# A gated delta-rule attention block and a top-1 column network on one core: the small matmuls in whole batches, gates and betas by Tanh, q and k scaled in place, a new order on all five engines

## The chip, the cores and the metric

One core of one Trainium2 chip. The metric is the device time of the kernel in microseconds. Engines are named as in the profile: PE is TensorE's matmuls, PEld its weight loads, DVE VectorE, ACT ScalarE, POOL GpSimd and SP SyncE, which issues nearly all transfers.

## The reference

Two residual layers over x of shape (4, 2048, 512), all in float32. The first is a recurrent attention with 16 heads of 32 channels, the second a network of 16 columns of which each token uses one.

```python
q, k, v, gate = ((x @ W.T).reshape(b, l, 16, 32) for W in (Wq, Wk, Wv, Wg))
beta = sigmoid(x @ Wb.T).reshape(b, l, 16, 32)
alpha = exp(-exp(A_log) * softplus(x @ Wa.T + dt_bias))          # one per head
q = q / norm(q) / sqrt(32);  k = k / norm(k)
def step(S, (k_t, q_t, v_t, beta_t, a_t)):                        # over time, S is 32x32 per head
    S = S * a_t
    S = S + k_t[:, None] * ((v_t - k_t @ S) * beta_t)[None, :]
    return S, q_t @ S
ctx = rmsnorm(ys) * norm_w * silu(gate);  attn = ctx @ Wo.T + bo
x = x + layernorm(attn(layernorm(x)))
logits = cosine(x, col_emb) + sigmoid(gelu(x @ gate_w1 + gate_b1) @ gate_w2 + gate_b2)
y = softmax weight of the best column * gelu(x @ W_cols[best] + b) @ proj_w[best] + proj_b + x
x = x + layernorm(layernorm(y) * ln_g + ln_b)                     # ffn of layernorm(x)
```

## The kernel before

**Stages.** A main stage goes through the sequence in 32 blocks of 64 time steps for all four batch rows, so 256 tokens a block. A second stage, after it, takes the tokens sorted by their column in 80 groups of 128 rows. The change is in the main stage.

**The main stage.** Each engine runs its own `step(...)` 35 times. A step holds work of four blocks at once: `chain` is the recurrence of block b, `ahead` the projections and decays of the next block, `after` the outputs of the one before, `late` the column choice of the one before that. 31 of the steps have both `chain` and `ahead`. The order of work in a step is written out by hand on each engine; semaphores join them.

**The recurrence** runs in two chunks of 32 time steps, with a state S of 32x32 for each of 16 groups (`G`) on each of four partition quarters, so 64 small products make one batch. There are six kinds: `key_products` (L469), `state_to_u` (L477), `first_half_to_u` (L485), `state_to_outputs` (L492), `chunk_to_outputs` (L497), `change_state` (L504). Each batch is issued in two halves of 32 products (`on_tiles(half, ...)`), and other PE work stands between most halves. Each product is a float32 matmul on a 32x32 part of the array and appears in the trace as two matmuls and two weight loads: a half is 64 matmuls, a batch is 128 matmuls and 128 weight loads. Between the products DVE solves a triangular system column by column (`solve_half`, L1145 to L1160), four times a step, and adds the state (`add_to_state`, L1165).

**Large matmuls.** `project` (L437) makes q, k, v, beta and gate from xT, with 256 columns each; `squares_sum` (L446), `decays` (L522), `log_alpha` (L511), `output_projection` (L535), `outputs_squares_sum` (L530), `turn` (L454, transposes), `gate_hidden` (L543), `gate_logits` (L553, L556) and `ranks` (L565 to L571) are the rest. They share three PSUM banks (`work`), given out in the order of the list `TURNS`: `into` makes PE wait until the bank's last use has been read (`READ_BY`).

**ACT** copies PSUM out: `copy_and_square` (L802, qraw and its square), `inverse_norm` (L809), `copy_decays` (L816), `copy_outputs` (L792, frees uq), `copy_turned` (L796), `copy_values` (L839). `sigmoid` (L835) makes beta and the gate's sigmoid `sg`, from another table than Ln and Exp; the statistics (`token_norm`, `length_of_normed`) and Gelu (L910) change tables again, each change an ACT_TABLE_LOAD. DVE multiplies `sg` by the gate in PSUM (L1281, L1290) and q and k by their inverse norms (`scale`, L1171).

**POOL** multiplies pairs of rows by beta (`pairs_times_beta`, L992), decays state, k and q (L976, L981, L1003), adds the residual (L1039) and scatters rows to DRAM (L1019). **SP** writes `Ak` to DRAM and fetches it back broadcast over partitions (`fetch_pairs`), loads tokens and stores outputs. Its queue order is `fetch_pairs(0,1)`, residual, `write_rows(1)`, `fetch_pairs(1,0)`, `fetch_pairs(1,1)`, `load_tokens`, `write_rows(0)`, `store`, `fetch_pairs(0,0)`.

## Time and profile before

| what | value |
| --- | --- |
| time, median of 3 runs | 3433.52 us (3429.26 to 3442.22) |
| the profiled execution's own time | 3454.87 us |
| its span in the profile | 3453.1 us |
| PE busy | 3006.9 us, 87% |
| PEld busy | 2295.4 us, 66% |
| DVE busy | 2357.6 us, 68% |
| ACT busy | 1824.4 us, 53% |
| POOL busy | 1913.1 us, 55% |
| mean granted clock of PE | 0.912 |

The span runs from the first to the last instruction. Busy times of engines overlap each other. PE and PEld are two sides of one engine: a weight load can run while a matmul does. In the profile, an idle time is followed by an arrow and what ended it; "issue" stands where the engine waited for nothing that the profile shows. The main stage fills the span from its first microseconds to about 3050 us.

### The profile page before, as it was taken

The page shows a single profiled execution, that of the slowest core. Times are in us where ns is not written, and L with a number is a line of the kernel's source. Part 1 is how long each engine was busy: PE and PEld are TensorE (multiplying, and loading weights), DVE is VectorE, ACT ScalarE, POOL GpSimd, SP SyncE. Part 2 cuts the span into 40 slices and gives each one's busy share as a digit, 9 for nine tenths or more (in the row PEclk, how much of TensorE's full clock was granted, in tenths as well). Part 3 has the DMA queues.
Part 4 walks back from the last instruction along what each step waited for, and adds up shares of the span by engine and source line. Part 5 has one row for each costly group of instructions (what it writes and reads, how often), then busy time and mean ns, then how long its engine had stood idle before and what let it go on. Part 6 is the DMA issues. An engine that isn't in the chain of part 4 may idle for free.

```text
span 3453.1 us, 141658 instructions
## 1 busy us (share of the span) xinstructions
PE 3006.9 (87%) x59368; PEld 2295.4 (66%) x59368; DVE 2357.6 (68%) x10708; ACT 1824.4 (53%) x4154; POOL 1913.1 (55%) x2903
## 2 busy tenths in 40 slices
PE   4899999999999999999999999999999999637774
PEld 4667777777777777777777777777777777414443
DVE  1667666666666766777666666666666677657896
ACT  2355555555555555555555555555555555326664
POOL 1555565455555555555565555555556555416887
PEclk9899999999999999999999999999999999759997
DMA  3544444544444445444444454444445444545773
GB/s 112 132 119 115 113 117 112 124 117 108 118 115 114 117 121 124 112 113 117 115 117 112 124 124 110 114 115 115 116 116 124 124 111 118 142 141 105 132 126 65
DMA packets 350030, 404.87 MB, mean 117 GB/s; under 512 B 31169, under 2 KB 293953, under 8 KB 348881
## 3 DMA queue, kind: packets, MB, share of 16 engines
q1 hardware_dynamic: 332752, 362.10, 42.1%
q0 software_dynamic: 16640, 33.71, 5.4%
q8 instruction: 468, 7.67, 1.0%
q14 instruction: 170, 1.38, 0.1%
HBM read 323.97 MB, written 75.93 MB: 116 GB/s over the span
## 4 chain that ended last, share of the span: by engine, by line
PE 62%; ACT 20%; DVE 11%; issue 4%; POOL 1%; ACTq 1%; DMA 1%; POOLq 0%; SPq 0%; DVEq 0%
PE work L437 25%; PE work L535 7%; PE work L543 3%; PE work L446 3%; DVE uk L1158 3%; DVE Ut L1155 3%; PE su L504 3%; PE work L454 2%; PE uq L497 2%; PE uk L477 2%; PE kkq L469 2%; PE uq L492 2%; PE work L530 2%; PE work L522 2%; PE work L511 2%
## 5 line engine op out<-in xcount | busy, mean ns | idle before, releaser
L437 PE MATMUL work<-xT,w_sb 128*128 128x256 f32 x5120 | 1314.1, 407 | 6.5 <-ACT beta L835 5.1
L992 POOL TENSOR_TENSOR pairs<-pairs,beta 128x240 f32<-128x240 f32 (+14 forms) x1920 | 862.4, 488 | 667.0 <-ACT beta L835 380.9
L437 PEld LDWEIGHTS work<-xT,w_sb 128*128 128x128 f32 x5120 | 996.3, 202 | 183.8 <-issue 31.1
L1158 DVE TENSOR_TENSOR uk<-uk,Ut 128x120 f32<-128x120 f32 (+14 forms) x3840 | 708.6, 226 | 1.1
L1155 DVE TENSOR_TENSOR Ut<-pairs,uk 128x120 f32<-128x120 f32 (+14 forms) x3840 | 688.2, 215 | 5.5 <-POOL pairs L992 5.0
L802 ACT ACTIVATE qraw<-work 128x512 f32<-128x512 f32 x128 | 75.9, 593 | 432.2 <-DVE kq L1171 305.5
L1165 DVE TENSOR_TENSOR S<-Sd,su 128x512 f32<-128x512 f32 x64 | 44.0, 687 | 359.1 <-PE su L504 359.1
L535 PE MATMUL work<-wo_sb,ctxT 128*128 128x512 f32 x512 | 240.6, 613 | 6.3 <-POOL ctxT L1011 6.3
L1003 POOL TENSOR_TENSOR kd<-kd,dec 128x512 f32<-128x512 f32 x64 | 68.0, 1084 | 258.8 <-DVE kd L1237 258.8
L492 PEld LDWEIGHTS uq<-kqd,S 32*32 32x32 f32 x8192 | 90.7, 114 | 156.8 <-ACT oT L792 105.8
L1145 DVE TENSOR_TENSOR uk<-vT,uk 128x128 f32<-128x128 f32 x256 | 62.9, 291 | 187.7 <-PE uk L485 115.8
L492 PE MATMUL uq<-kqd,S 32*32 32x32 f32 x8192 | 105.6, 203 | 95.7 <-ACT oT L792 93.4
L809 ACT ACTIVATE qr<-work 128x512 f32<-128x512 f32 x128 | 75.9, 593 | 193.9 <-PE work L446 191.5
L1017 POOL TENSOR_TENSOR xfw<-xfw,pb_sb 128x1024 f32<-128x1024 f32 x32 | 75.5, 2359 | 175.7 <-DVE slot L1224 175.7
L535 PEld LDWEIGHTS work<-wo_sb,ctxT 128*128 128x128 f32 x512 | 93.7, 193 | 105.4 <-issue 94.8
L1171 DVE TENSOR_TENSOR kq<-qraw,qr 128x512 f32<-128x512 f32 x128 | 136.1, 1082 | 35.0 <-ACT qr L810 35.0
L839 ACT ACTIVATE vT<-work 128x512 f32<-128x512 f32 x64 | 38.2, 597 | 224.5 <-PE work L437 224.5
L981 POOL TENSOR_TENSOR kqd<-kq,eg 128x1024 f32<-128x1024 f32 x64 | 150.3, 2349 | 3.8 <-DVE kq L1171 3.8
L976 POOL TENSOR_TENSOR Sd<-S,eg_end 128x512 f32<-128x512 f32 x64 | 67.9, 1061 | 148.6 <-DVE S L1165 148.6
L446 PE MATMUL work<-qsq,squares 128*128 128x512 f32 x256 | 147.0, 658 | 0.0
L469 PEld LDWEIGHTS kkq<-kq 32*32 32x32 f32 x8192 | 119.1, 105 | 34.1 <-issue 29.8
L1194 DVE TENSOR_TENSOR lt<-work,gb_sb 128x32 f32<-128x32 f32 x32 | 6.1, 191 | 195.7 <-PE work L556 195.7
(249 smaller groups left out, 5970.8 us busy)
## 6 DMA issues: line engine op xcount, KB each, us to landing
pairs<-pair_rows SPq DMA_DIRECT2D x512, 256.0 KB, 3.5
pairs<-pair_rows SPq DMA_DIRECT2D x512, 224.0 KB, 3.7
xt<-in_x SPq DMA_DIRECT2D x66, 256.0 KB, 5.4
pair_rows<-Ak SPq DMA_DIRECT2D x64, 256.0 KB, 2.3
x<-in_x SPq DMA_DIRECT2D x64, 256.0 KB, 4.8
out<-x SPq DMA_DIRECT2D x64, 256.0 KB, 3.7
wo_sb<-xs_rows SPq DMA_DIRECT2D x30, 258.0 KB, 2.9
w_sb<-in_w_in SPq DMA_DIRECT2D x1, 5120.0 KB, 14.9
```

The lines of the kernel that those rows point to most:

```text
L437: mm = pe.matmul(w[:, half * BT:(half + 1) * BT], w_sb[:, f, j * D + hg * P:j * D + (hg + 1) * P], xT[:, f, :], start=(f == 0), stop=(f == ...
L446: pe.matmul(w, blk1, qsq[n % 2][:], start=True, stop=True).then_inc(s["ss_full"], 1)
L469: on_tiles(half, "kkq_full", lambda g, q, q_half: pe.matmul(kkq[q, g], kq[q, g, c, 0, :], kq[q, g, c].rearrange("p a t -> p (a t)"), start ...
L492: on_tiles(half, None, lambda g, q, q_half: pe.matmul(uq[q, g], S[q, g, :], kqd[c][q, g, 1, :], start=(g == 0), stop=True, skip_group_chec ...
L504: on_tiles(half, "su_full", lambda g, q, q_half: pe.matmul(su[q, g, :], kd[c][q, g, :], delT[c][q, g, :], start=True, stop=True))
L535: mm = pe.matmul(w, flat(ctxT[:, hg * B + tb * BL:hg * B + (tb + 1) * BL, :]), wo_sb[:, hg, :], start=(hg == 0), stop=(hg == KD - 1))
L543: mm = pe.matmul(w[:, n * BT:(n + 1) * BT], gw1_sb[:, f, n * P:(n + 1) * P], xfT[:, f, :], start=(f == 0), stop=(f == KD - 1))
L981: link(nc.gpsimd.tensor_tensor(kqd[c][:], kq[:, :, c], eg[:, :, c * C:(c + 1) * C].unsqueeze(2).to_broadcast([P, G, 2, C]), ALU.mult), "kq ...
L992: ins = nc.gpsimd.tensor_tensor(a, a, beta[:, :, t:t + WID[t0]], ALU.mult)
L1155: link(v.tensor_tensor(Ut[:, g, 0:n], pr[:, g], uk[:, g, at:at + 1].to_broadcast([P, G // 2, n]), ALU.mult), "vb_free" if i and (c, j, t0) ...
L1158: link(v.tensor_tensor(uk[:, g, at + 1:at + 1 + n], uk[:, g, at + 1:at + 1 + n], Ut[:, g, 0:n], ALU.subtract), f"pairs_free{j}" if i and t ...
L1171: link(v.tensor_tensor(unit(kq, hp)[:, :, :, 1 - j, :], per_chunk(qraw[n % 2][:]), per_chunk(qr[n % 2][:]), ALU.mult), "kq_ready", hold=(n ...
```

## The change

- **PE.** `on_tiles` loses its halves: each kind is one batch of 64 products. In a step the batches stand in four runs: `change_state(1)`, `chunk_to_outputs(1)` at the end of a step and `state_to_u(0)`, `key_products(1)`, `state_to_outputs(0)` at the start of the next, five in a row; `first_half_to_u(0)` alone; `change_state(0)`, `chunk_to_outputs(0)`, `state_to_u(1)`, `state_to_outputs(1)`, four in a row; `first_half_to_u(1)`, `key_products(0)`, two in a row. The number of products stays. `chunk_to_outputs(1)` moves to its own step. `TURNS` is reordered, and alpha lies in the bank of the logits.
- **ACT.** One change to the table with Tanh and Gelu and one back in each step. Sigmoid becomes 0.5 * tanh(x/2) + 0.5 for beta (two instructions for each half); the gate is copied to `silu`, its tanh goes to `xn`, and DVE makes (tanh + 1) * gate, with the missing half put into `nw`. q and k go from PSUM straight into `kq`; new waits guard `kq`, `dec`, `xn` and `beta` (for beta, all of POOL's pair products of the block).
- **DVE.** `scale` works in place in `kq`; the decays are turned from `dec`, which takes the place of `gsb`; `decay_products(0)` stands inside `solve_half(1, 1)`; other parts are reordered.
- **POOL.** The decay differences go ahead of the scatter, and half of the last pair products ahead of the residual.
- **SP.** `load_tokens` goes ahead of `fetch_pairs(1,1)`, `store` ahead of `write_rows(0)`.

```diff
-    ("logits",), ("xT", 0), ("xT", 1), ("qk", 0), ("rms", 0), ("rms", 1), ("alpha",), ("qk", 1), ("ss", 0),
-    ("qk", 2), ("wo", 0), ("wo", 1), ("rank",), ("ss", 1), ("G", 0), ("G", 1), ("qk", 3), ("ss", 2),
-    ("gate", 0), ("ss", 3), ("gate", 1), ("beta", 0), ("beta", 1), ("xfT", 0), ("xfT", 1), ("v", 0), ("v", 1),
-    ("hid",),
+    ("xT", 0), ("xT", 1), ("rms", 0), ("rms", 1), ("qk", 0), ("logits",), ("qk", 1), ("ss", 0), ("qk", 2), ("ss", 1),
+    ("G", 0), ("G", 1), ("wo", 0), ("wo", 1), ("rank",), ("ss", 2), ("qk", 3), ("gate", 0), ("ss", 3), ("gate", 1),
+    ("beta", 0), ("beta", 1), ("xfT", 0), ("xfT", 1), ("v", 0), ("v", 1), ("hid",),
 ]
 BANK = {use: n % NW for n, use in enumerate(TURNS)}
+BANK["alpha",] = BANK["logits",]
...
+   rank="rank_read", gate="gate_read", beta="beta_read", v="v_read", xfT="xfT_ready", hid="h_ready",
...
-        qraw = [sb(f"qraw{n}", [P, GU * T]) for n in range(2)]
         qsq = [sb(f"qsq{n}", [P, GU * T]) for n in range(2)]
-        qr = [sb(f"qr{n}", [P, GU * T]) for n in range(2)]
-        sg = sb("sg", [P, GU * T])
+        qr = [sb(f"qr{n}", [P, GU * T]) for n in range(4)]
...
-        gsb = qsq[1][:], ctx_flat[:, 0:GU * T]
-        gT = qraw[1][:], ctx_flat[:, GU * T:2 * GU * T]
+        gT = gate_t = [xn[:, hp, :] for hp in range(2)]
...
+    if ahead:
+        load_tokens(following)
+    if chain:
         fetch_pairs(1, 1)
-    if ahead:
-        load_tokens(following)
...
-def on_tiles(half, full, product):
-    for g in range(half * GU, (half + 1) * GU):
+def on_tiles(product):
+    for g in range(G):
         for h in range(HP):
             mm = product(g, slice(DH * h, DH * h + DH), slice(DH * h, DH * h + CS))
-    if half and full:
-        mm.then_inc(s[full], 1)
...
-def state_to_u(c, half):
-    if not half:
-        take(pe, "kqd_ready")
-        take(pe, "S_ready")
-    on_tiles(half, "uk_full", lambda g, q, q_half: pe.matmul(
-        uk[q, g], S[q, g, :], kqd[c][q, g, 0, :], start=(g == 0), stop=True, skip_group_check=True))
...
+    take(pe, "kqd_ready")
+    take(pe, "S_ready")
+    on_tiles(lambda g, q, q_half: pe.matmul(
+        uk[q, g], S[q, g, :], kqd[c][q, g, 0, :], start=(g == 0), stop=True, skip_group_check=True))\
+        .then_inc(s["uk_full"], 1)
...
 def step(p, chain, after, ahead, late):
     if chain:
-        state_to_u(0, 0)
-    if late:
-        gate_logits(0)
-    if chain:
-        state_to_u(0, 1)
-    if late:
-        gate_logits(1)
+        state_to_u(0)
+        key_products(1)
+        state_to_outputs(0)
     if ahead:
         take(pe, "xn_ready", TB)
         turn("xT", xn, 0)
         turn("xT", xn, 1)
     if after:
-        chunk_to_outputs(NC - 1, 0)
-        chunk_to_outputs(NC - 1, 1)
+        outputs_squares_sum(0)
+        outputs_squares_sum(1)
     if ahead:
         take(pe, "xT_ready", 2)
         project("qk", 0, 0, 0)
+    if late:
+        gate_logits(0)
+    if ahead:
         project("qk", 0, 0, 1)
-    if chain:
-        key_products(1, 0)
-        key_products(1, 1)
-    if after:
-        outputs_squares_sum(0)
-        outputs_squares_sum(1)
-    if ahead:
-        log_alpha(0)
-    if chain:
-        first_half_to_u(0, 0)
-    if ahead:
-        log_alpha(1)
+    if late:
+        gate_logits(1)
+    if ahead:
+        log_alpha(0, late)
+        log_alpha(1, late)
         project("qk", 0, 1, 0)
+        project("qk", 0, 1, 1)
+    if chain:
+        first_half_to_u(0)
+    if ahead:
...
-    if chain:
-        first_half_to_u(0, 1)
-    if ahead:
-        project("qk", 0, 1, 1)
         project("qk", 1, 0, 0)
-    if chain:
-        state_to_outputs(0, 0)
-    if after:
-        take(pe, "ctx_ready", 2)
-        output_projection(0)
-    if chain:
-        state_to_outputs(0, 1)
-    if ahead:
         project("qk", 1, 0, 1)
-    if chain:
-        change_state(0, 0)
-    if after:
-        output_projection(1)
-    if chain:
...
         squares_sum(1)
         take(pe, "lax_ready")
         decays(0)
         decays(1)
-    if chain:
-        state_to_u(1, 0)
-    if ahead:
+    if after:
+        take(pe, "ctx_ready", 2)
+        output_projection(0)
+        output_projection(1)
+    if chain:
+        change_state(0)
+        chunk_to_outputs(0)
+        state_to_u(1)
+        state_to_outputs(1)
+    if late:
+        ranks()
+    if ahead:
+        squares_sum(2)
         project("qk", 1, 1, 0)
-    if chain:
-        state_to_u(1, 1)
-    if ahead:
         project("qk", 1, 1, 1)
-        squares_sum(2)
...
         project("gate", 4, 0, 0)
-    if chain:
-        chunk_to_outputs(0, 0)
-    if ahead:
+        project("gate", 4, 0, 1)
         squares_sum(3)
-        project("gate", 4, 0, 1)
-    if chain:
-        chunk_to_outputs(0, 1)
-    if ahead:
         project("gate", 4, 1, 0)
         project("gate", 4, 1, 1)
+    if chain:
+        first_half_to_u(1)
+    if ahead:
         take(pe, "kq_ready", 4)
-        key_products(0, 0)
+        key_products(0)
         project("beta", 3, 0, 0)
-        key_products(0, 1)
         project("beta", 3, 0, 1)
-    if chain:
-        first_half_to_u(1, 0)
-    if ahead:
         project("beta", 3, 1, 0)
-    if chain:
-        first_half_to_u(1, 1)
+        project("beta", 3, 1, 1)
...
-    if ahead:
-        project("beta", 3, 1, 1)
-    if chain:
-        state_to_outputs(1, 0)
-    if after:
         turn("xfT", xfw, 1)
     if ahead:
         project("v", 2, 0, 0)
-    if chain:
-        state_to_outputs(1, 1)
-    if ahead:
         project("v", 2, 0, 1)
+    if ahead:
         project("v", 2, 1, 0)
-    if chain:
-        change_state(1, 0)
+        project("v", 2, 1, 1)
     if after:
         take(pe, "xfT_ready", 2)
         gate_hidden()
     if chain:
-        change_state(1, 1)
-    if ahead:
-        project("v", 2, 1, 1)
+        change_state(1)
+        chunk_to_outputs(1)
...
+def load_tanh_gelu():
+    nc.scalar.preload_act_table_set("gelu_and_others")
...
-    take(act, "kq_ready", free=2)
+    j, hp = divmod(n, 2)
     take(act, "qk_full")
-    nc.scalar.activation(qraw[n % 2][:], bank("qk", n), ACT.Copy)
+    nc.scalar.activation(unit(kq, hp)[:, :, :, 1 - j, :], per_chunk(bank("qk", n)), ACT.Copy)
     link(nc.scalar.activation(qsq[n % 2][:], bank("qk", n), ACT.Square), "q_sq_ready")
...
-    link(nc.scalar.activation(gsb[hp], w, ACT.Copy), "g_copied")
+    link(nc.scalar.activation(flat(unit(dec, hp)), w, ACT.Copy), "g_copied")
...
-def sigmoid(name, hp, dst):
-    take(act, name + "_full")
-    return nc.scalar.activation(dst, bank(name, hp), ACT.Sigmoid)
+def copy_gate(p, hp):
+    take(act, "gate_full")
+    link(nc.scalar.activation(flat(unit(silu[1 - p], hp)), bank("gate", hp), ACT.Copy), "gate_read", hold=True)
+def gate_tanh(p, hp):
+    nc.scalar.activation(gate_t[hp], flat(unit(silu[1 - p], hp)), ACT.Tanh, scale=0.5).then_inc(s["gate_ready"], 1)
+def beta_sigmoid(hp):
+    b = flat(unit(beta, hp))
+    take(act, "beta_full")
+    link(nc.scalar.activation(b, bank("beta", hp), ACT.Tanh, scale=0.5), "beta_read", hold=True)
+    link(nc.scalar.activation(b, b, ACT.Identity, scale=0.5, bias=half[:]), "beta_ready")
...
     if ahead:
+        take(act, "gate_used", 2, free=2)
         norm_tokens(xn, xt, x_rn, "xn_ready")
+    if after:
+        square_outputs(0)
+        square_outputs(1)
+    if ahead:
         copy_turned("xT", xT, 0)
         copy_turned("xT", xT, 1)
-    if late:
-        take(act, "lg_ready")
-        nc.scalar.activation(lt[:, 1], lt[:, 1], ACT.Exp, scale=-1.0).then_inc(s["sig_ready"], 1)
-    if after:
-        copy_outputs(NC - 1)
-        square_outputs(0)
-        square_outputs(1)
-    if ahead:
-        copy_and_square(0)
     if after:
         inverse_rms(0)
         inverse_rms(1)
...
-    if after:
-        take(act, "ctx_raw", 2)
-    if ahead:
+        take(act, "kt_ready", 2, free=2)
+        take(act, "kqd_ready", 2, free=2)
+        copy_and_square(0)
+    if late:
+        take(act, "lg_ready")
+        nc.scalar.activation(lt[:, 1], lt[:, 1], ACT.Exp, scale=-1.0).then_inc(s["sig_ready"], 1)
+    if ahead:
+        copy_and_square(1)
         inverse_norm(0)
-        copy_and_square(1)
         copy_and_square(2)
+        inverse_norm(1)
+        take(act, "kd_ready", 2, free=2)
+        copy_decays(0, 1 - p)
+        copy_decays(1, 1 - p)
...
+    if after:
+        take(act, "ctx_raw", 2)
+    if chain:
+        copy_outputs(0)
+    if ahead:
+        inverse_norm(2)
+        copy_and_square(3)
     if after:
         take(act, "y_mv_ready")
         token_norm(y_rn, y_mv)
...
         pair_decays(1)
-        inverse_norm(2)
+        copy_gate(p, 0)
         inverse_norm(3)
-        take(act, "gate_used", free=1)
-        link(sigmoid("gate", 0, sg[:]), "gate_ready")
-        take(act, "gate_used", free=1)
-        link(sigmoid("gate", 1, sg[:]), "gate_ready")
+        copy_gate(p, 1)
...
     if after:
         take(act, "x1_mv_ready")
         token_norm(x1_rn, x1_mv)
         norm_tokens(xfw, x1, x1_rn, "xf_ready")
-        length_of_normed(x1_mv, x1_rn)
-    if chain:
-        copy_outputs(0)
-    if after:
-        copy_turned("xfT", xfT, 0)
+    if ahead:
+        take(act, "x_mv_ready")
+        token_norm(x_rn, x_mv)
+    load_tanh_gelu()
     if ahead:
         if chain:
             take(act, "vb_free")
-        link(sigmoid("beta", 0, flat(unit(beta, 0))), "beta_ready")
-        link(sigmoid("beta", 1, flat(unit(beta, 1))), "beta_ready")
+            take(act, "pr_ready", 8)
+        beta_sigmoid(0)
+        beta_sigmoid(1)
...
+        gate_tanh(p, 0)
+        gate_tanh(p, 1)
+    if after:
+        copy_turned("xfT", xfT, 0)
+        copy_turned("xfT", xfT, 1)
+    if ahead:
         copy_values(0)
-    if after:
...
             link(nc.scalar.activation(hT[n], bank("hid")[:, n * BT:(n + 1) * BT], ACT.Gelu, bias=gb1_sb[:, n:n + 1]), "h_ready")
+    if chain:
+        copy_outputs(1)
     load_ln_exp()
-    if ahead:
-        copy_values(1)
-        take(act, "x_mv_ready")
...
+def pairs_times_beta(c, j, parts=(0, 1)):
+    for n in parts:
...
+    if chain:
+        decay_state(p, 1)
+        pairs_times_beta(1, 1, (0,))
...
-        decay_state(p, 1)
-        pairs_times_beta(1, 1)
+        pairs_times_beta(1, 1, (1,))
...
-        link(v.tensor_tensor(uk[:, g, h], uk[:, g, h], beta[:, g, th], ALU.mult), behind=1)
+    for i, g in enumerate(turns):
+        link(v.tensor_tensor(uk[:, g, h], uk[:, g, h], beta[:, g, th], ALU.mult),
+             "vb_free" if i and (c, j) == (NC - 1, 1) else None, behind=1, hold=True)
...
-    link(v.tensor_tensor(unit(kq, hp)[:, :, :, 1 - j, :], per_chunk(qraw[n % 2][:]), per_chunk(qr[n % 2][:]), ALU.mult), "kq_ready", hold=(n == 1))
+    link(v.tensor_tensor(unit(kq, hp)[:, :, :, 1 - j, :], unit(kq, hp)[:, :, :, 1 - j, :], per_chunk(qr[n][:]), ALU.mult), "kq_ready")
...
+def gate_values(p, hp):
+    half_silu = flat(unit(silu[1 - p], hp))
+    take(dve, "gate_ready")
+    link(v.scalar_tensor_tensor(half_silu, gate_t[hp], 1.0, half_silu, ALU.add, ALU.mult), "gate_used")
...
+        normed_outputs(1)
     if ahead:
...
-    if ahead:
-        take(dve, "kqd_ready", 2, free=2)
...
+    if ahead:
+        for hp in range(2):
+            take(dve, "g_copied")
+            link(v.transpose(gT[hp], flat(unit(dec, hp))), "gT_ready")
...
+    if after:
+        for tb in range(TB):
+            token_stats(y, y_mv, tb, "y_mv_ready")
     if ahead:
         scale(1)
-        take(dve, "g_copied")
-        link(v.transpose(gT[0], gsb[0]), "gT_ready")
-        take(dve, "g_copied")
...
-        take(dve, "gate_ready")
-        link(v.tensor_tensor(flat(unit(silu[1 - p], 0)), bank("gate", 0), sg[:], ALU.mult), "gate_used")
...
     if ahead:
+        next_tokens_stats()
+    if ahead:
         take(dve, "dec_ready", 2)
+    if chain:
+        take(dve, "corr_full")
+        solve_half(1, 1, {2: lambda: decay_products(0)} if ahead else {})
+    elif ahead:
         decay_products(0)
-        take(dve, "gate_ready")
-        link(v.tensor_tensor(flat(unit(silu[1 - p], 1)), bank("gate", 1), sg[:], ALU.mult), "gate_used")
-        next_tokens_stats()
-    if chain:
-        take(dve, "corr_full")
-        solve_half(1, 1)
+    if ahead:
+        gate_values(p, 0)
+        gate_values(p, 1)
+    if chain:
         add_to_state()
...
```

## Rows read from the trace of the kernel before

**Rows 1.** The page, busy time of each engine over the span

```profile
PE 3006.9 (87%) x59368; PEld 2295.4 (66%) x59368; DVE 2357.6 (68%) x10708; ACT 1824.4 (53%) x4154; POOL 1913.1 (55%) x2903
```

**Rows 2.** Windows: one step; us, busy of each engine, PEclk, DMA share, GB/s

```profile
1506.24:1598.30 92.06, 84.71 (x1829) 65.92 (x1821) 63.87 (x316) 50.50 (x112) 51.51 (x78) 0.94 0.47 116
```

**Rows 3.** Waits over the whole span: us in total, times, longest us

```profile
DVE S L1165 <- PE su L504: 359.1, 33, 12.2
...
PE uq L492 <- ACT oT L792: 93.4, 31, 3.4
...
PE work L454 <- ACT beta L835: 46.6, 30, 1.8
...
PE uk L477 <- issue: 26.0, 52, 1.7
```

**Rows 4.** Timeline of PE: start us, us, instruction, idle before

```profile
1517.26 1.89 PE L437 MATMUL work<-xT,w_sb 128*128 128x256 f32 x8
1519.08 0.75 PE L497 MATMUL uq<-Aq,delT 32*32 32x32 f32 x64
1519.76 1.12 PE L446 MATMUL work<-qsq,squares 128*128 128x512 f32 x2
...
1529.82 1.10 PE L469 MATMUL kkq<-kq 32*32 32x64 f32 x64
1530.85 1.99 PE L437 MATMUL work<-xT,w_sb 128*128 128x256 f32 x8
1532.77 0.73 PE L485 MATMUL uk<-Ak,delT 16*32 16x16 f32 x64
...
1573.06 1.99 PE L469 MATMUL kkq<-kq 32*32 32x64 f32 x128
1574.97 1.99 PE L530 MATMUL work<-y,squares 128*128 128x512 f32 x4
```

**Rows 5.** Timeline of PEld in a middle step

```profile
1563.06 0.97 PEld L553 LDWEIGHTS work<-ceT,xfT 128*128 128x128 f32 x8 [1.07 <-issue]
1563.95 0.53 PEld L556 LDWEIGHTS work<-gw_sb,pairs 128*128 128x128 f32 x4
1564.31 1.55 PEld L454 LDWEIGHTS work<-squares,xn 128*128 128x128 f32 x8
1566.19 1.57 PEld L497 LDWEIGHTS uq<-Aq,delT 32*32 32x32 f32 x108 [0.33 <-issue]
1569.10 0.27 PEld L497 LDWEIGHTS uq<-Aq,delT 32*32 32x32 f32 x20 [1.33 <-issue]
```

**Rows 6.** Timeline of PEld in the last `chain` step

```profile
2946.04 0.73 PEld L497 LDWEIGHTS uq<-Aq,delT 32*32 32x32 f32 x76 [0.21 <-issue]
2946.67 0.10 PEld L469 LDWEIGHTS kkq<-kq 32*32 32x32 f32 x1
2946.68 0.10 PEld L497 LDWEIGHTS uq<-Aq,delT 32*32 32x32 f32 x1
2946.68 0.79 PEld L469 LDWEIGHTS kkq<-kq 32*32 32x32 f32 x50
2950.06 1.04 PEld L469 LDWEIGHTS kkq<-kq 32*32 32x32 f32 x48 [2.59 <-issue]
```

**Rows 7.** DMA queues in that middle step: packets, MB, share of 16 engines

```profile
q8 instruction: 14, 0.23, 1.1%
```

**Rows 8.** Windows beside a clock change, columns as in rows 2

```profile
1561.10:1564.55 3.45, 2.49 (x80) 2.35 (x80) 0.00 (x0) 2.90 (x8) 3.45 (x7) 1.00 0.86 192
1564.55:1567.97 3.42, 3.35 (x116) 2.89 (x115) 3.25 (x19) 1.31 (x3) 3.42 (x10) 0.50 0.55 118
...
2980.00:3000.00 20.00, 5.08 (x241) 4.33 (x241) 16.08 (x95) 8.54 (x29) 13.95 (x21) 0.53 0.72 191
```

**Rows 9.** Lines: table loads of ACT; busy us, mean ns, idle before

```profile
L835 ACT ACT_TABLE_LOAD x62 | 79.5, 1283 | 16.4 <-PE work L437 15.8
```

**Rows 10.** Timeline of DVE: first and last instructions of one `solve_half`

```profile
1514.71 0.49 DVE L1145 TENSOR_TENSOR uk<-vT,uk 128x128 f32<-128x128 f32 x2 [1.86 <-PE uk L477]
...
1523.97 0.72 DVE L1160 STREAM_TRANSPOSE delT<-uk 128x512 f32<-128x512 f32 x1
```

153 lines of the change are left out of this document (70 added, 83 removed).

## The prediction

> **What bounds the kernel now.** I read the busy shares first [rows 1]: PE leads with 87%, DVE has 68%, ACT and POOL under 56%. The windows view of one middle step (from one `ranks` to the next) gives 92.06 us with 84.71 busy on PE [rows 2]; DVE works 63.87 of it, ACT 50.50, POOL 51.51. So a step costs PE's work plus 7.35 us in which PE stands still. The waits show where other engines have room: DVE stood 359.1 us before the state add, waiting for PE, while PE's own large waits are 93.4 us before `state_to_outputs` (uq not yet copied by ACT) and 46.6 us before the transposes of xfw (a bank not yet read by ACT's sigmoid) [rows 3]. What sets the end of each step is PE, in program order.
>
> The next question is what small batches cost. In PE's timeline a half batch takes 0.68 us from its first matmul to the next work (1519.08 to 1519.76) and a `key_products` half 1.03 (1529.82 to 1530.85) [rows 4]. A whole batch is 1.36 and 1.91 us (1573.06 to 1574.97). That is 256 PE instructions in 1.4 to 1.9 us, and they must be brought in. The queue that carries instructions moved 14 packets, 0.23 MB, in the step, 16 KB each [rows 7], for 1829 + 1821 = 3650 matmuls and weight loads [rows 2]: one packet for 3650 / 14 = 261, so 256 with the few other instructions that PE has. The stalls called "issue" lie at exactly this distance. After the stall that ends at 1563.06 there come 8 + 4 + 8 + 108 = 128 weight loads, so 256 instructions, and then PEld stands 1.33 us until 1569.10 in the middle of a batch [rows 5]. In the last `chain` step, where the large matmuls between are missing, the same is seen bare: from 2946.04 PEld does 76 + 1 + 1 + 50 = 128 loads and stands 2.59 us until 2950.06, a period of 4.02 us for 256 instructions, in the middle of `key_products` [rows 6]. I read this as follows: the packet after next is asked for only when PE enters the next one, and takes about 4 us to be usable. Small batches between large matmuls hide it; 14 packets in 92 us is one in 6.6 us on average. Small batches in a row would not.
>
> **The change, part by part, for one of the 31 full steps.**
>
> *Switches between small and large work, gained.* A `key_products` batch in one piece saves 2 x 1.03 - 1.91 = 0.15 us. Eight large matmuls behind a small batch take 1.92 us (1530.85 to 1532.77), behind a large one 1.82 (1517.26 to 1519.08) [rows 4], so 0.10 more. Each switch out and back costs 0.25. Before there are 22 stretches of small work in a step (ten batches in two pieces, two in one), after it 4, so 18 x 0.25 = 4.5 us. Bounds: 1.8 us with only the 0.10, 6 us if the smaller batches save more than the wide one.
>
> *PE's waits, gained.* 93.4 / 31 = 3.0 us for uq: `chunk_to_outputs` now has a whole batch or two behind it before `state_to_outputs`, which covers ACT's copy. 46.6 / 31 = 1.5 us for the bank, as its reader moves. 26.0 / 31 = 0.8 us of "issue" at `state_to_u` [rows 3], counted anew below. Together 5.3; bounds 0.8 and 7.35, all idle time [rows 2].
>
> *Instructions, lost.* A batch is exactly one packet. In a run of n batches n packet borders are crossed; the packet behind the first was fetched during slow work, the other n - 1 must wait. The runs are 5, 1, 4 and 2 batches: 4 + 0 + 3 + 1 = 8 waits. Each packet takes 4.02 us [rows 6] in place of the batch's own 1.36, or 1.91 for the two `key_products` among them: 6 x 2.66 + 2 x 2.11 = 20.2 us. Bounds for one wait: 1.33 us, the stall seen in a middle step [rows 5], so 10.6 a step; above, 6.04 - 1.36 = 4.7, if the 6.04 us between the two stalls of that step were all fetch, so 37. Nothing at all is a rival. I take the bare period since it has little slow work in it, as the new runs have.
>
> *Clock, lost.* The granted clock fell to 0.50, the 1.2 GHz level, in the stretch behind one that had small batches and a stall in it (PE busy 2.49 of 3.45), and stood at 0.53 over 20 us with PE busy 5.08 [rows 8]. Starved runs of 20, 16 and 8 us will be at the low level; small batches don't feel it, but the large matmuls just behind each run do, for one or two such stretches of 3.4 us, at half speed: 1.7 to 3.4 us, three times, 5 to 10. The step already loses some: a mean of 0.94 [rows 2] is (1 - 0.94) x 92 / 0.5 = 11 us at the low level, some 4 us of it lost in dense work. Net +3; bounds 0 and +7.
>
> *Dependences.* Inside a run the state add (0.7 us on DVE) and ACT's copy of uq are behind a 4 us packet, so they cost nothing; without the starvation the state add after `change_state` is still covered by the 1.36 us of `chunk_to_outputs`, nearly. A `solve_half` takes 1514.71 to 1524.69, 10.0 us [rows 10]. Between `state_to_u(0)` and `first_half_to_u(0)` PE now has two batches and some 15 us of large work; between `state_to_u(1)` and `first_half_to_u(1)` one batch and 14 us, where DVE also has `rows_of_tokens`, two token statistics and a scale ahead of the solve: about even. I book +1 for it. The beta wait on all eight pair products holds ACT, with xfT, v and the hidden layer queued behind; PE has 15 us of `first_half_to_u`, `key_products` and beta before the bank, so nothing, up to 3 us.
>
> *ACT.* Some 6 table loads fewer, 1.283 us each [rows 9], against two gate copies and two more passes for beta: it is not what ends a step, so nothing beyond the waits above. In-place scaling, the dec turn on DVE and the new SP order are likewise off PE's path: DVE has 28 us free a step [rows 2]. `load_tokens` now goes ahead of `fetch_pairs(1,1)` and waits for the decays, `write_rows(0)` waits behind the store; both stand ahead of pair products needed more than 10 us later. Zero, up to 2 us.
>
> Sum: -4.5 - 5.3 + 20.2 + 3 + 1 = +14.4 us a step, x 31 = +446. The second stage and the ends are untouched. The profiled execution took 3454.87 us, so 3901; the median of the runs is 0.994 of that execution (3433.52 / 3454.87), so about 3875.
>
> **The rivals.**
>
> *Instructions are not what binds (faster).* PE gets packets early enough in the new runs, either since it holds more than two or since they can overlap. Then a step is 92.06 - 4.5 - 5.3 + 1 = 83.3: 31 x -8.8 = -273, so 3182, 3162 as a median. For it: in most of the step's borders nothing is lost, and `issue` is only 26.0 us at `state_to_u` [rows 3]. Against it: two stalls 256 instructions apart [rows 5, 6], each in the middle of a batch where no semaphore is. The point from which it decides is a period of about 2.4 us for a packet: 8 waits of (2.4 - 1.5) would be all that the gains of 8.8 allow beside the clock. The Trainium skill states this rival as a rule (Runtime: NRT & Kernel Launch, Instruction fetch mechanics): PE's instruction memory holds 2048 instructions, refilled in blocks of 256, and the refill is mostly hidden. By that rule a run of 1280 instructions would be in store and the sum would be this rival's; the trace agrees with the block of 256 and not with the depth. 10%.
>
> *A smaller wait (slower by less).* The wait is 1.33 us as in the middle step [rows 5]: 10.6 in place of 20.2, a step of +4.8, +149 in all, 3582 as a median. 10%.
>
> *Gains and losses cancel.* Waits of 1.33 us, no clock loss and the upper bound of the switches give -6 - 5.3 + 10.6 + 1 = 0.3 a step. 5%.
>
> **How the numbers follow.** The forecast, waits near 2.5 us each, has 75%. The range takes in the smaller wait and reaches 3560 below; above, 5 us a step over the forecast for slower packets in a busy step and the clock's upper bound, so 4050. A measurement of this kernel can tell about 0.5% from no change. Slower 75 + 10, same 5, faster 10.
>
> **What would show it.** A step (one `ranks` to the next) near 106 us; weight loads of the runs in pieces of 128, each begun 4 us behind the last with an idle time of 2 to 2.7 us put down to "issue"; eight of them a step; uq's wait on ACT gone; granted clock below 0.9 in the middle; still 14 instruction packets a step; eight table loads down to two. I am wrong if whole batches follow each other at 1.4 us, or if a wait of PE on DVE or POOL over 3 us stands in every step.

## The result, and the profile after

The changed kernel takes 3838.53 us (median of 4 runs, 3828.82 to 3844.84) against 3435.88 us (3429.26 to 3442.22) for the kernel before: a ratio of 1.117 [1.1137, 1.1202]. It is slower by about 400 us, and the forecast was 3875. A step of the main stage, from one `ranks` to the next, takes 104.7 us in the mean of the middle ones, where it took 92.2: 12.5 us more, and 31 such steps are 388 us. So nearly all of it comes from the steps, and they are read below. The trace of the kernel before is of an execution of 3454.87 us, 19 us above this median (0.6 us a step), so the 12.5 us are low by about that much.

The page's busy times and granted clock, the kernel after:

```profile
PE 3059.7 (80%) x59368; PEld 2459.9 (64%) x59368; DVE 2357.2 (61%) x10710; ACT 1657.7 (43%) x4103; POOL 1903.2 (50%) x2903
PEclk9788888888888887788888888887888888767998
...
PE 69%; issue 15%; DVE 9%; ACT 4%; POOL 1%; ACTq 1%; DMA 0%; DVEq 0%; POOLq 0%
```

PE is the busiest still, and it is busy 53 us longer than in [rows 1], but its share fell from 87% to 80% because the span grew. The last line, the chain that ended last by engine, gives 15% to "issue", time in which an engine waits for nothing that the profile shows. No other engine became the bound: all shares fell.

PE's waits name what the idle time is. Engine, line and what it waited for: us in total, times, longest. First the main part of the main stage (548.6 to 3250 us, 25.8 steps):

```profile
PE uk L473 <- issue: 114.7, 51, 3.4
PE uq L493 <- issue: 114.1, 48, 4.5
PE uq L488 <- issue: 95.5, 50, 3.8
PE kkq L465 <- issue: 83.1, 48, 2.9
PE kkq L465 <- DVE kq L1158: 6.9, 6, 1.7
```

The first four rows are 407.4 us in 197 stalls: 7.6 stalls a step, 2.07 us each, 15.8 us a step; with two small rows more, at L528 and L481, "issue" is 16.0 us a step, where it was 1.1. All four stand at lines of small batches. What another engine causes is 0.6 us a step. The waits for ACT's copy of uq and for the bank, 4.5 us a step before [rows 3], have no row left that counts; with the wait for the next tokens' norm, what PE waited for ACT was 5.0 us a step before.

Where a stall stands is seen in the weight loads of the run of four batches (start, us, the group, idle time before):

```profile
1589.65 1.16 PEld L501 LDWEIGHTS su<-delT,kd 32*32 32x32 f32 x127 [0.76 <-issue]
...
1590.73 0.76 PEld L493 LDWEIGHTS uq<-Aq,delT 32*32 32x32 f32 x75
1593.66 0.73 PEld L493 LDWEIGHTS uq<-Aq,delT 32*32 32x32 f32 x50 [2.17 <-issue]
...
1594.30 1.11 PEld L473 LDWEIGHTS uk<-kqd,S 32*32 32x32 f32 x73
1597.84 0.78 PEld L473 LDWEIGHTS uk<-kqd,S 32*32 32x32 f32 x51 [2.42 <-issue]
...
1601.58 0.83 PEld L488 LDWEIGHTS uq<-kqd,S 32*32 32x32 f32 x53 [1.95 <-issue]
```

The three long idle times (2.17, 2.42, 1.95 us) are inside batches, where no semaphore is. Between the first and the second there are 50 + 2 + 2 + 73 = 127 weight loads, and a record can be missing: 256 instructions, as in [rows 5, 6]. The stretches begin 4.18 and 3.74 us apart. Over 24 middle steps there are 108 such distances inside runs, 3.36 to 5.95 us, 4.07 in the mean. The run of five, in PE's own timeline, has four:

```profile
1543.06 0.70 PE L493 MATMUL uq<-Aq,delT 32*32 32x32 f32 x36 [2.22 <-issue]
...
1547.91 0.70 PE L473 MATMUL uk<-kqd,S 32*32 32x32 f32 x36 [2.93 <-issue]
...
1553.58 1.18 PE L465 MATMUL kkq<-kq 32*32 32x64 f32 x36 [2.53 <-issue]
...
1557.05 0.76 PE L488 MATMUL uq<-kqd,S 32*32 32x32 f32 x39 [1.01 <-issue]
...
1559.50 3.62 PE L528 MATMUL work<-y,squares 128*128 128x512 f32 x4
```

The last row stands behind the run, with only eight transposes between: four matmuls of 512 columns in 3.62 us, where the same four took 1.99 us before [rows 4]. That is the clock. The windows view gives it by stretch: the whole step, the run of five, the stretch behind it, the work up to the run of four, that run, the stretch behind it. Columns: us; busy time of PE, PEld, DVE, ACT, POOL; granted clock; DMA share; GB/s.

```profile
1497.60:1602.47 104.87, 87.47 (x1812) 71.13 (x1810) 63.35 (x314) 44.84 (x110) 51.79 (x78) 0.81 0.42 102
1538.79:1557.73 18.94, 10.25 (x641) 9.58 (x640) 9.62 (x63) 5.28 (x8) 10.58 (x21) 0.60 0.48 111
1557.73:1563.04 5.31, 5.31 (x20) 3.24 (x14) 3.61 (x9) 2.51 (x4) 2.11 (x2) 0.50 0.24 57
1563.04:1589.65 26.61, 26.61 (x253) 20.00 (x251) 15.22 (x84) 13.15 (x36) 9.88 (x18) 1.00 0.44 106
1589.65:1602.47 12.82, 6.64 (x513) 6.21 (x512) 3.30 (x7) 0.60 (x1) 5.01 (x4) 0.66 0.54 131
1602.47:1607.41 4.94, 4.94 (x19) 3.63 (x15) 2.73 (x10) 1.02 (x2) 1.94 (x1) 0.50 0.03 6
```

The full 26.61 us without a gap, large work but for the one batch `first_half_to_u(0)`, run at 1.00. The two starved runs take 31.8 us of the step for 16.9 busy ones, and each is followed by some 5 us of dense work at 0.50, the 1.2 GHz level. The step's mean clock is 0.81, against 0.94 in [rows 2].

### The profile page after: what moved, and what is told of

Read it like the earlier page. It is cut to its first block, busy times and chain, and to the rows that moved or that the text cites. A ratio compares the mean times of both kernels' runs of the same rounds, so it can differ in the third digit from the quotient of the medians.

```text
span 3836.3 us, 141487 instructions
## 1 busy us (share of the span) xinstructions
PE 3059.7 (80%) x59368; PEld 2459.9 (64%) x59368; DVE 2357.2 (61%) x10710; ACT 1657.7 (43%) x4103; POOL 1903.2 (50%) x2903
## 4 chain that ended last, share of the span: by engine, by line
PE 69%; issue 15%; DVE 9%; ACT 4%; POOL 1%; ACTq 1%; DMA 0%; DVEq 0%; POOLq 0%
PE work L435 27%; PE work L533 6%; PE kkq L465 5%; PE uq L488 3%; PE work L541 3%; PE uk L473 3%; PE work L444 3%; PE uq L493 2%; PE work L452 2%; PE work L528 2%; PE su L501 2%; PE uk L481 2%; DVE uk L1145 2%; DVE Ut L1142 2%; PE work L509 1%
## 5 line engine op out<-in xcount | busy, mean ns | idle before, releaser
L435 PE MATMUL work<-xT,w_sb 128*128 128x256 f32 x5120 | 1250.4, 403 | 6.1 <-ACT beta L811 2.5
L435 PEld LDWEIGHTS work<-xT,w_sb 128*128 128x128 f32 x5120 | 1034.6, 204 | 243.7 <-issue 88.4
L977 POOL TENSOR_TENSOR pairs<-pairs,beta 128x240 f32<-128x240 f32 (+14 forms) x1920 | 861.8, 485 | 662.5 <-DMA pairs<-pair_rows 662.2
L465 PE MATMUL kkq<-kq 32*32 32x64 f32 x8192 | 221.1, 282 | 107.8 <-issue 99.7
L465 PEld LDWEIGHTS kkq<-kq 32*32 32x32 f32 x8192 | 197.2, 151 | 123.5 <-issue 112.1
L473 PE MATMUL uk<-kqd,S 32*32 32x32 f32 x8192 | 126.0, 223 | 146.4 <-issue 142.8
L1004 POOL TENSOR_TENSOR dec<-dec,xn 128x512 f32<-128x512 f32 x64 | 81.8, 1278 | 323.3 <-DVE xn L1259 323.3
L493 PE MATMUL uq<-Aq,delT 32*32 32x32 f32 x8192 | 106.5, 204 | 148.3 <-issue 148.3
L473 PEld LDWEIGHTS uk<-kqd,S 32*32 32x32 f32 x8192 | 112.3, 136 | 155.0 <-issue 151.3
L493 PEld LDWEIGHTS uq<-Aq,delT 32*32 32x32 f32 x8192 | 93.2, 114 | 152.1 <-issue 152.0
L767 ACT ACTIVATE kq<-work 128x512 f32<-128x512 f32 x128 | 75.8, 592 | 234.9 <-PE work L435 234.7
```

Of the source, the lines that this page charges most:

```text
L435: mm = pe.matmul(w[:, half * BT:(half + 1) * BT], w_sb[:, f, j * D + hg * P:j * D + (hg + 1) * P], xT[:, f, :], start=(f == 0), stop=(f == ...
L465: on_tiles(lambda g, q, q_half: pe.matmul(kkq[q, g], kq[q, g, c, 0, :], kq[q, g, c].rearrange("p a t -> p (a t)"), start=True, stop=True))\
L473: on_tiles(lambda g, q, q_half: pe.matmul(uk[q, g], S[q, g, :], kqd[c][q, g, 0, :], start=(g == 0), stop=True, skip_group_check=True))\
L493: on_tiles(lambda g, q, q_half: pe.matmul(uq[q, g], delT[c][q, g, :], Aq[c][q, g, :], start=False, stop=True, skip_group_check=True))\
L977: ins = nc.gpsimd.tensor_tensor(a, a, beta[:, :, t:t + WID[t0]], ALU.mult)
L1004: link(nc.gpsimd.tensor_tensor(d, d, gT[hp], ALU.subtract))
```

## The experiments

The theory: PE's instructions arrive in packets of 256, one ahead, and the next takes 3.5 to 4 us to be usable; batches in a row need one in every 1.4 us. The rivals: the new order on the other engines holds PE up, whole batches are slower in themselves, or the packets wait behind the data traffic. Every kernel was timed with the kernel before on the same chip, and only those ratios are compared. `spread` with `before_whole`, `supply` and `supply_traffic` ran on one chip (before: 3454.77 us), the rest on another (3433 us). One kernel's ratio still differed by 1.3% between the two (`before_whole`), so a difference of ratios below that isn't read across them.

**Spread: all of the change, but no two batches in a row.** The edit moves calls of PE's step, and three calls of ACT and DVE so that their waits stay covered. The four runs become twelve single batches with large work between.

```diff
     if chain:
         state_to_u(0)
-        key_products(1)
-        state_to_outputs(0)
...
+    if chain:
+        key_products(1)
...
+    if chain:
+        state_to_outputs(0)
...
     if chain:
         change_state(0)
-        chunk_to_outputs(0)
+    if after:
+        output_projection(1)
+    if chain:
         state_to_u(1)
-        state_to_outputs(1)
...
+    if chain:
+        change_state(1)
     if ahead:
         project("v", 2, 1, 0)
         project("v", 2, 1, 1)
+    if chain:
+        chunk_to_outputs(1)
...
-    if chain:
-        change_state(1)
-        chunk_to_outputs(1)
...
```

> The changed kernel with its whole batches kept, but no two of them in a row: 3 to 7 us of large matmuls stand between any two (ACT's two copies of uq and one DVE addition move along). Supply theory (PE gets 256 instructions, one batch, per 3.5 to 4 us, and stalls when it needs them sooner): the idle time put down to issue falls from 15.9 us a step to under 2, a step from 104.7 us to 84 to 90, the whole to 3200 to 3400 us. Rival (what costs is the new work on ACT and DVE and its waits, not the rows of batches): the step stays above 98 us, the whole above 3630.

Measured: 3375.31 us, 0.9775 [0.9748, 0.9802] of the kernel before, a step of 89.9 us. The loss of 11.7% became a gain of 2.2% with every operation kept. Its batches are whole and in one piece in the timeline, and its waits (500 to 2850 us, 26.1 steps) are of another kind:

```profile
1598.66 1.29 PE L473 MATMUL uk<-kqd,S 32*32 32x32 f32 x128
...
1606.99 1.99 PE L465 MATMUL kkq<-kq 32*32 32x64 f32 x128
```

```profile
PE work L452 <- ACT xn L726: 61.1, 26, 2.6
PE uk L481 <- DVE delT L1156: 43.0, 25, 2.6
PE work L452 <- ACT beta L820: 21.4, 17, 2.2
PE uk L473 <- issue: 17.3, 19, 2.2
```

"Issue" at small and large lines together is down to 1.7 us a step. In its place stand waits for the norm of the next tokens (2.3 us a step), for the solve (1.6 and more) and for the bank (0.8). Together the waits for other engines are 5.5 us a step, as much as in the kernel before (5.0) and far above the 0.6 of the change, where a late PE hides them.

**Before, whole batches in the old order.** This is the half that the change was to win from.

```diff
 def on_tiles(half, full, product):
-    for g in range(half * GU, (half + 1) * GU):
+    if not half:
+        return
+    for g in range(G):
```

> The kernel before, with nothing changed but that the first half of each small batch is issued with its second half: 12 stretches of small work a step in place of 22, each still between large matmuls. If a switch costs 0.25 us as the prediction worked out: 10 x 0.25 = 2.5 us a step, 78 in all, about 3358 us (ratio 0.977). If a switch costs nearly nothing, as the balance of the changed kernel's step suggests: 0 to -0.7 us a step, ratio 0.993 to 1.00. If whole batches already meet the supply limit here: slower.

> The kernel before with whole batches once more, for its trace, since its time was the same as before (1.0014). If a switch really costs 0.25 us, PE's small batches take 2.5 us a step less and another wait has grown by as much. If a switch costs nothing, batches and large matmuls take the same time as before, and no wait has changed.

> The kernel before with whole batches, timed again, as the first time (1.0014) and the look's step (90.2 us against 92.2) disagree. The look's trace: small batches 2.5 to 3.3 us a step less, the wait for uq gone (3.0), the wait for xfT's bank up from 1.5 to 5.9. If the look was right: ratio 0.975 to 0.985. If the gain is only moved: 0.995 to 1.003.

Measured: on the first chip 3462.98 us, 1.0014 [0.9996, 1.0031], just above the range that was given for a switch that costs nothing; on the second 3396.64 us in a single run (before 3433.08) and 3398.44 us in five rounds, 0.9888 [0.9868, 0.9909], between the two ranges expected. The two chips differ by 1.3%. On the second, the profile of the five-round kernel (500 to 2850 us) has

```profile
PE work L454 <- ACT beta L837: 150.3, 26, 6.2
PE uk L479 <- issue: 16.9, 17, 2.2
```

The uq wait of [rows 3] is gone (3.0 us a step) and the bank wait rose from 1.5 to 5.8 us, because PE arrives there earlier. All of PE's waits together are 8.0 us a step (6.1 before), and the step is 90.4 us, so PE's own work is 82.4 us in place of 86.0. Of these 3.6 us, 1.0 is clock (large matmuls spend 6.4 us a step at the low level, before 8.4). The other 2.6 us are put down to the ten switches that this kernel leaves out (12 stretches of small work for 22), 0.26 each. That is an upper estimate: the trace of the kernel before is of an execution of 3454.87 us, 21 us above the 3433.63 of this chip, 0.7 us a step; without it 0.19 is left for each. Why the first chip shows no gain stays open, since no comparable profile of this kernel is at hand from there.

**Supply: the same series of instructions alone.** This kernel computes something else: PE multiplies one loaded tile, eight batches of 64 small products with 0, 2, 4, 8 and 16 large products behind each, and no other engine works meanwhile. Its second form lets SP load 2 MB at a time without a pause.

```diff
+BIG = (0, 2, 4, 8, 16)
+ROUNDS = 8
...
+            for n in BIG:
+                large(40)
+                for _ in range(ROUNDS):
+                    batch()
+                    if n:
+                        large(n)
```

> Another computation: five series of 8 small batches (128 matmuls and 128 weight loads each, no semaphore inside), with 0, 2, 4, 8 and 16 large float32 products of 256 columns behind each batch, 40 of them ahead of each series, and no other transfer. Supply theory: at 0 a batch comes every 3.5 to 4.0 us, at 2 (about 0.9 us of large work) the same, at 4 still about 4, at 8 (3.6 us) it is the work itself, 5.1, and at 16 8.8; ahead of a series two packets are in store, so the first stall comes after one to two batches. Rival (PE or its memory is slow on small matmuls in a row, or more packets are held than two): at 0 a batch takes 1.4 us, or the first eight do.

Measured, from the end of one stall to the end of the next: 3.45 to 3.73 us at 0 large products (3.56 in the mean of five), 3.45 to 4.00 at 2 (3.77 of six), 3.45 to 3.73 at 4 (3.54 of six). At 8 large products a batch and what follows it take 4.87 us and at 16 they take 8.32, without a stall. The weight loads at 0, then at 8:

```profile
23.46 2.44 PEld L56 LDWEIGHTS small<-a 32*32 32x32 f32 x272 [0.33 <-issue]
28.18 1.18 PEld L56 LDWEIGHTS small<-a 32*32 32x32 f32 x128 [2.28 <-issue]
...
157.44 1.18 PEld L56 LDWEIGHTS small<-a 32*32 32x32 f32 x128 [0.33 <-issue]
158.66 3.32 PEld L60 LDWEIGHTS big<-a 128*128 128x128 f32 x16
```

After 40 large products the first 272 loads, 544 instructions, come freely: the rest of a packet and what was fetched. From there on every 128 loads, 256 instructions, cost 3.45 to 4.00 us, whatever fills them: at 2 and 4 large products the large work is nearly free. Counted through all 6080 weight loads of the run, each of its 15 stalls over 0.36 us after the start stands at 96 more than a multiple of 128. Nor does the period follow the clock: the 128 loads take 1.18 us at the high level and 1.80 at the low one (granted clock 0.50 from 31.6 to 35.0 us), and both periods are 3.45 us; the slower batch only leaves a shorter stall. No semaphore, no transfer of data and no other engine is in this, so the packet explains the stall by itself. At 8, 288 instructions take 4.87 us, 4.3 us for 256, and nothing is lost. The two readings bound the point on a quiet chip: under 3.45 us of work for 256 instructions PE stands, at 4.3 it does not.

**Supply under traffic.** The edit turns the loads on.

```diff
-TRAFFIC = False
+TRAFFIC = True
```

> The same with 2 MB loads issued one behind the other by SP all the time. If the time of a packet is mostly its own round trip: the period at 0 grows by under 15%. If it waits behind other transfers: over 4.5 us, which would make the 4.7 us periods of the changed kernel's steps a matter of its data traffic.

Measured, beside some 238 GB/s of loads: from stall to stall 4.96 us in the mean at 0 large products (single periods 3.73 to 6.75), and for 256 instructions 5.5 at 2 and 5.3 at 4. From one batch's start to the next it is 6.31 in the mean at 8 (4.87 without a stall, single ones 8.21 and 11.6), and 8.32 at 16, as without traffic.

```profile
37.47 1.80 PEld L56 LDWEIGHTS small<-a 32*32 32x32 f32 x128 [4.95 <-issue]
41.20 1.80 PEld L56 LDWEIGHTS small<-a 32*32 32x32 f32 x128 [1.93 <-issue]
47.39 1.79 PEld L56 LDWEIGHTS small<-a 32*32 32x32 f32 x128 [4.40 <-issue]
```

The first of these loads begins 6.75 us behind the one before it, the second 3.73: nearly the quiet period comes back between longer ones. So the packets do wait behind data: 4.96 us against 3.56 is 39% more in the mean of the bare series. It explains why the periods of the changed kernel, at 102 GB/s, reach 5.95 us and are 4.07 in the mean, but not the loss: 3.45 to 4.00 us are there with no traffic. By the two means traffic has 0.5 us of each stall of the change, an estimate.

**Pairs: the batches of `spread` in six runs of two.** It asks whether the number of batches in a run matters, or each border in it. ACT's `copy_outputs(0)` goes back to its place in the change.

```diff
     if chain:
         state_to_u(0)
+        key_products(1)
...
     if chain:
+        state_to_outputs(0)
         first_half_to_u(0)
...
         change_state(0)
+        chunk_to_outputs(0)
...
         state_to_u(1)
+        state_to_outputs(1)
...
         first_half_to_u(1)
...
+        key_products(0)
...
         change_state(1)
+        chunk_to_outputs(1)
...
```

> The spread kernel with its twelve batches in six runs of two in a row. Supply theory, one packet in store beyond the current one: in most runs the second batch stalls once, 4 to 6 stalls of 2.1 us a step, 8 to 12.6 us, ratio to the kernel before 1.05 to 1.09, between spread (0.9775) and the changed kernel (1.117). If only long runs stall (more in store): under 3 us of issue a step, ratio under 1.00.

Measured: 3864.21 us, 1.124 [1.1171, 1.1309], as slow as the change and above the 1.05 to 1.09 expected. Waits of 500 to 2850 us (22.2 steps), and PE's timeline behind one pair:

```profile
PE uq L493 <- issue: 126.6, 39, 5.1
PE kkq L465 <- issue: 96.6, 40, 3.4
PE uq L488 <- issue: 61.2, 21, 4.3
PE uk L481 <- issue: 49.1, 21, 3.2
```

```profile
1609.42 0.96 PE L488 MATMUL uq<-kqd,S 32*32 32x32 f32 x53 [3.08 <-issue]
...
1612.04 2.06 PE L444 MATMUL work<-qsq,squares 128*128 128x512 f32 x2
1613.89 8.18 PE L435 MATMUL work<-xT,w_sb 128*128 128x256 f32 x32
1621.90 1.02 PE L444 MATMUL work<-qsq,squares 128*128 128x512 f32 x2
```

Four to six stalls of 2.1 us a step were expected, and 5.9 are there, so each border counts. But a stall is 2.7 us here and 2.07 in the change. Only 4.3 us a step of small work is at the low level here, 12.6 in the change, so the batches may be done sooner and leave more of the packet's time idle, as in `supply`; that is argued, not shown. And there are six stretches behind a run instead of three: the same two matmuls take 2.06 us right behind the pair and 1.02 us later. Large matmuls spend 21.2 us a step at the low level (8.4 in the kernel before, 12.5 in the change), so (21.2 - 8.4) / 2 = 6.4 us go to the clock beside 15.8 us to the stalls. Fewer borders did not help, for both reasons.

**One fetch outstanding.** If the packets of the change wait behind SP's transfers, fewer of these in flight should shorten the stalls.

```diff
-OUTSTANDING = 2
+OUTSTANDING = 1
...
-                for odd in range(2):
+                for odd in range(2 - OUTSTANDING, 2):
```

> The changed kernel with one pair transfer under way at a time in place of two (OUTSTANDING = 1). If packets of instructions wait behind SP's transfers, as the test with 2 MB loads showed, the mean stall of a run falls from 2.1 us towards 1.9, the value of the quiet test (3.45 less the batch), 1 to 2 us a step, 1.10 to 1.115. If packets take their own 3.5 us anyway: ratio 1.115 to 1.12. If the pair products come late instead, POOL and DVE wait and it is slower than 1.12.

Measured: 4019.64 us, 1.1708 [1.1686, 1.1729]. Its "issue" waits fall to 292.1 us in 154 stalls, 1.90 us each (2.07 in the change), and new waits stand beside them (500 to 2850 us):

```profile
PE kkq L465 <- DVE kq L1158: 53.7, 18, 6.7
PE work L520 <- POOL xt L992: 48.7, 20, 7.8
```

POOL's wait for the pairs that arrive by DMA rose from 662.2 to 1849.3 us in the whole span. The stalls are a little shorter, but PE is waiting for POOL and DVE now, so the run only bounds what fewer fetches under way can give: less than 0.2 us of a stall.

**Sigmoid in place of Tanh.** One more table load a step; it asks what the ACT part of the change is worth.

```diff
-nc.scalar.activation(gate_t[hp], flat(unit(silu[1 - p], hp)), ACT.Tanh, scale=0.5).then_inc(s["gate_ready"], 1)
+nc.scalar.activation(gate_t[hp], flat(unit(silu[1 - p], hp)), ACT.Sigmoid).then_inc(s["gate_ready"], 1)
...
-link(nc.scalar.activation(b, bank("beta", hp), ACT.Tanh, scale=0.5), "beta_read", hold=True)
-link(nc.scalar.activation(b, b, ACT.Identity, scale=0.5, bias=half[:]), "beta_ready")
+link(nc.scalar.activation(b, bank("beta", hp), ACT.Sigmoid), "beta_read", hold=True)
+link(nc.scalar.activation(b, b, ACT.Copy), "beta_ready")
...
-load_tanh_gelu()
...
```

> The spread kernel with Sigmoid in place of Tanh for gates and betas and a table load more in each step (1.28 us on ACT); the number of instructions stays, beta's second pass is a copy. If ACT ends nothing, as the prediction has it: within 0.3% of spread. If the tables were worth what the change's words suggest: a load on the path of beta and the transposes behind it, 1.3 us a step, 40 us, ratio up by 0.012.

Measured: 3388.82 us, 0.9896 [0.9862, 0.993], against 0.9775 for `spread` on the other chip, a difference no larger than the 1.3% between chips. The wait of PE for the norm of the next tokens is the better witness:

```profile
PE work L452 <- ACT xn L726: 90.9, 26, 3.9
```

It was 61.1 us in `spread`: (90.9 - 61.1) / 26 = 1.15 us more a step, nearly the 1.28 us of one load [rows 9]. That would be 36 us in 31 steps; the ratios differ by 41 us, and how much of these is the chip's isn't known. In the spread order the table load at the end of the step lies on PE's way.

**Two further versions.** `spread2` moves the hidden layer ahead of the last value projection, so that Gelu and the table change behind it end earlier, ACT's last copy of values behind the next tokens' norm, and the gate's tanh ahead of beta's, with the gate's product at column 6 of the last solve. `spread3` puts the tanh behind beta's again and the product at column 11.

```diff
+    take(pe, "xfT_ready", 2)
+    gate_hidden()
 if chain:
     chunk_to_outputs(1)
+if ahead:
+    project("v", 2, 1, 0)
+    project("v", 2, 1, 1)
...
-    solve_half(1, 1, {2: lambda: decay_products(0)} if ahead else {})
+    solve_half(1, 1, {2: lambda: decay_products(0), 6: lambda: [gate_values(p, hp) for hp in range(2)]} if ahead else {})
...
```

> The spread kernel with two of its own waits taken away: PE waits 2.4 us a step for the normed tokens (ACT makes them after Gelu and a table load); the hidden layer now goes ahead of the last value projection, whose copy follows the tokens' norm, and the gate's tanh and its product on DVE move ahead so that xn is free. If these waits set the step: 89.9 to about 87.5 us, the whole 70 to 80 us under spread, ratio to the kernel before 0.955. If PE only finds its next wait (DVE's solve, the bank of xfT behind ACT's beta): 0 to 25 us gained, ratio 0.97 to 0.978.

> The second spread kernel with the gate's tanh behind beta's and its product at column 11 of the solve in place of 6, so that the bank of xfT is read 1.15 us sooner. If that bank's wait (1.8 us a step) sets PE: ratio 0.972 to 0.96. If DVE's solves are next in line (their wait is 2.5 us a step): within 0.3% of 0.972.

Measured: 3331.14 us, 0.9722 [0.9692, 0.9751], and 3330.3 us, 0.9719 [0.9672, 0.9766]: the same time. In `spread2` the wait for xn is gone; from there to `spread3` the bank wait went down and DVE's solve, which has the gate's product in it, came up by as much:

```profile
PE work L452 <- ACT beta L820: 36.7, 21, 3.3
PE su L501 <- DVE delT L1157: 20.4, 14, 3.1
```

```profile
PE su L501 <- DVE delT L1157: 40.2, 26, 2.2
PE work L452 <- ACT beta L820: 15.7, 14, 2.3
```

(The first fence is `spread2`, the second `spread3`, both 500 to 2850 us.) These two are the best versions seen: 2.8% faster than the kernel before and 13% faster than the change, (1 - 0.972 / 1.117). What they gain over `spread` (0.9775 on the other chip) is less than the chips differ.

## Why the prediction was right, point by point

**What bounds it.** PE in program order, and a packet of 256 instructions at each border of a run: shown by the 128-load distance in the change, by `spread`, which took the loss away with nothing but another order of the calls, and by `supply`, which has the stalls without any other engine. The rival that instructions do not bind would have put the step at 83.3 us and needed batches 1.4 us apart; it fell. By the Trainium skill (Runtime: NRT & Kernel Launch, Instruction fetch mechanics) PE's instruction memory holds 2048 instructions and refills are mostly hidden. By that rule a run of five batches, 1280 instructions, would have cost nothing; in the runs here it holds 544 at most ahead of a stall.

**The instruction term.** Forecast were +20.2 for the runs, less the 0.8 of "issue" that stood before: +19.4. Measured is +14.9, 16.0 now less 1.1. The count was right (7.6 of 8 stalls a step). The size was off: 2.07 us for a stall, not 2.53. The period was not what made it too high: 4.02 us were taken from one bare stall [rows 6], and the mean in the change is 4.07, which is luck in part, since single periods are 3.36 to 5.95 us and those of quiet `supply` 3.45 to 4.00. What was wrong is the batch inside it. The sum booked 1.50 us for it in the mean (1.36, and 1.91 for `key_products`), and 4.07 less an idle time of 2.1 leaves 2.0 (see the next point but one). A longer batch leaves less of the period to stand: some 0.45 us in each of 7.6 stalls, 3.4 of the 4.5 us.

**PE's other waits.** Forecast -4.5, 3.0 for uq and 1.5 for the bank. Measured -4.4, from 5.0 to 0.6 us a step. For uq the reason holds without a late PE too: its wait is gone in `before_whole_again`, which only makes the batches whole, and doesn't come back in `spread`. For the rest the late PE is the cover: in `spread`, whose order is a little different, 5.5 us a step of waits stand at xn, the solve and the bank.

**Switches and clock.** Forecast -4.5 and +3, so -1.5 for PE's own work. Measured is +2.1: the step without its waits went from 86.0 to 88.1 us. This is the step that failed. The clock's part on large matmuls is (12.5 - 8.4) / 2 = +2.0, within its bounds. The switches seem to exist too, 0.19 to 0.26 us each in `before_whole_again` for 0.25 booked, on one of two chips. But "small batches don't feel it", said of the low level, is wrong:

```profile
1619.90 0.41 PE L465 MATMUL kkq<-kq 32*32 32x64 f32 x12
1621.98 3.41 PE L465 MATMUL kkq<-kq 32*32 32x64 f32 x116 [1.67 <-issue]
```

The windows of these 116 matmuls and of the whole batch in `spread` (the granted clock is the third number from the end):

```profile
1621.98:1625.39 3.41, 3.41 (x117) 3.24 (x116) 3.27 (x15) 3.21 (x14) 1.70 (x1) 0.50 0.02 7
1606.99:1608.90 1.91, 1.91 (x129) 1.82 (x128) 1.91 (x18) 1.85 (x6) 1.91 (x5) 1.00 0.58 152
```

This `key_products` batch of the change takes 0.41 + 3.41 = 3.8 us without its stall, against 1.91 in [rows 4] and 1.99 in `spread`. Of the 32x32 kinds, 88 matmuls took 1.40 us in the run of five, 16 ns each; the whole batch in `spread` took 1.29 us, 10 ns each. Summed over PE's records without waits, small batches take 21.9 us a step, 12.6 of them at the low level; before it was 18.9 with 2.7, in `spread` 16.7 with 0.3. So the low level costs small batches some 5 us a step, which the sum had at nothing. Large work takes 66.0 us where it took 67.1, though the clock takes 2 us more of it, so the gain of the switches is there and is eaten.

**Dependences.** Forecast +1. The solve costs PE 0.1 us a step (3.2 us at L481 in 25.8 steps), so nothing. For a PE that is not starved it is 1.6 us a step at that line, in `spread`: the 1 us that was booked, nearly.

**ACT.** Forecast nothing beyond the waits above. Its table loads fell from 251 to 72 and its busy time by 167 us. No run takes the tables alone out of the change, so that they are worth nothing there isn't shown; a PE that is late waits for ACT only 0.1 us a step. As a general statement it is wrong: the chain from Gelu over the table change to xn ends a wait of PE in `spread` and `spread_sigmoid`.

**The sum.** Measured +14.9 - 4.4 + 2.1 makes +12.6 of the 12.5 us found; forecast +19.4 - 4.5 - 1.5 + 1 = +14.4. The total came nearer than its parts: an instruction term 4.5 too high stands against 3.6 that switches and clock did not give. Most of this is one error seen twice, and no luck: the packet sets the pace, so what a batch loses to the clock its stall gives back. The signs that were named are there: a step of 104.7 us for 106, pieces of 128 loads some 4 us apart, 7.6 stalls for 8, a clock of 0.84 over the middle steps, 13 instruction packets in the step shown for 14.
